# Two graph attention layers on one core: the uniform rows of two stages computed in one pair of records and spread through memory, with another order of the adjacency loads

## The chip, the cores and the metric

One core of one Trainium2 chip. The time is device microseconds of one execution; the median of several runs counts. Line numbers as L850 are lines of the kernel before. Stages are numbered from 0 to 15, and "late in stage 14" is a place in that numbering.

## What is computed

Eight graphs (B = 8) with 1024 nodes and 128 features each go through two layers. In each layer the features are normalised over a row, clipped at zero, projected with a 128 x 128 matrix, and combined by attention over the neighbours that the adjacency matrix (1.6% ones, int32) names; the result is added to the input. Layer 0 puts an ELU on the result, layer 1 doesn't.

```python
h  = maximum(layernorm(x), 0)
Wh = h @ W                                   # [8, 1024, 128]
e  = leaky_relu(Wh @ a1 [:, :, None] + Wh @ a2 [:, None, :], 0.2)
p  = softmax(where(adj > 0, e, very_negative), axis=2)
x  = x + elu(p @ Wh)                         # layer 1: x + p @ Wh
```

## The kernel before

**Stages.** A stage is one layer of one graph; 0 to 7 are layer 0, 8 to 15 (LAST) are layer 1. All engines run hand-written programs with semaphores between them, and work on neighbouring stages at once. While the matrix engine (PE) sums the attention of stage n, the projection of n+1 is made and the transposes of n+2.

**PE in stage n** (L954 to 961): `project(n + 1)`, eight matmuls of 130 columns (L850) and one more (L853) which multiplies the sum of the rows of h, repeated over 128 columns, by W; `attend(n, (0,))`, eight matmuls (L911) for mask 0; `spread_emax`, one transpose (L858); masks 1 to 5; eight transposes of stage n+2 (L789); masks 6 and 7. An f32 matmul is two records in the trace, so x16 is eight matmuls.

**Masks.** For each of the eight 128 x 1024 tiles of the adjacency VectorE (DVE) makes one operand of a matmul (L666): the larger of a row `row_r` that is the same on all partitions and a scalar, cut to the 0 or 1 of the adjacency by a minimum. To every sum a **uniform row** is added: `EMPTY` (2^-112) times the sum of all rows of Wh, so small that it counts only for a node without neighbours, whose softmax is uniform. Its first 128 columns are what L853 computes, on all partitions at once, into the free end of a bank of `prj` (`USUM`); DVE scales them into `uniform[:, m % 2, 0:D]` in `copy_e` (L602), and `copy_acc` (L675) of the same stage adds them as it moves the sums out of PSUM. A bank is free for PE's next stage only after that copy (`acc_copied`, waited for at L908).

**The row.** `row_r` of stage m comes from `sqr` (128 x 8, written by ScalarE, ACT, in `exps`), early in stage m-1: SP writes it to the DRAM tensor `r_rows` (L217), waits for that, and reads it back on all partitions as `row_by_node` (L222); ACT then puts it into the order of the masks with a stride of 8 elements (`sort_row`, L423), and DVE waits for that before mask 0 (L665). On ACT the copy `copy_hT(n + 2)` (L381), which the next `project` waits for, stands behind `sort_row`. Stage 1 alone does without memory (`SPREAD`).

**SP's queue.** One queue issues nearly all transfers, in the order written at L228 to 266, and stops at each wait. In iteration n it issues the adjacency tiles AHEAD (5) to 7 of stage n+1, the row's write and read (`load_row`), x of graph n+4 while there is one, tiles 0 to 4 of stage n+2, and in layer 1 the store of a finished graph. In iteration 1 tiles 5 to 7 come behind the row. The adjacency has three slots of eight tiles, and a load waits for the mask that used its tile three stages earlier.

**DVE in stage n** (L752 to 769): masks 0 and 1, `take_acc(n - 1)` (the three copies L675 and a reciprocal), `copy_e(n + 1)`, mask 2, `exp_args(n + 1)`, masks 3 to 5, the ELU and residual work, masks 6 and 7, statistics of n+3. Stage 15 has masks 0 and 1, `take_acc(14)`, then the rest.

## Time and profile before

| what | value |
|---|---|
| median of 3 runs | 296.29 us (295.84 to 296.66) |
| the profiled execution, its own time | 297.17 us |
| its span | 295.2 us |
| PE busy | 287.5 us, 97% of the span |
| DVE busy | 259.2 us, 88% |
| ACT busy | 190.5 us, 65% |
| the DMA queue that SP issues to | 82.78 MB, 74.4% of 16 engines |
| granted clock of PE | 1.0 of full speed |

The profiled execution took 0.88 us more than the median; the part of it outside the span (1.97 us) is launch and end. The page shows the span in equal slices, the chain of work that ended last, and groups of instructions. The trace behind it can be asked for the waits, the chain in order of time, a timeline by engine and busy time in windows.

### The profile page before, as it was taken

Reading aid. Unit: us, or ns where it says so; the run is one execution under the profiler, and the core shown is the slowest. Engines: PE = TensorE matmul, PEld = TensorE weight load, DVE = VectorE, ACT = ScalarE, POOL = GpSimd, SP = SyncE. Lnnn points to the kernel's source line nnn. Section 1 sums busy time; section 2 is a strip of 40 time slices with the busy share of each in tenths; the row PEclk is TensorE's granted clock in tenths of the full one; section 3 lists DMA queues with packets and bytes.
Section 4 is the critical chain, followed back from the end, with each engine's and each line's share of the span. In section 5 each row is a group of like instructions: output and inputs, shape, how many; then the busy total and the mean of one; then the engine's idle time right before and its main releaser. Section 6 shows DMA issues by size and latency. Waiting matters only on the chain.

```text
span 295.2 us, 6658 instructions
## 1 busy us (share of the span) xinstructions
PE 287.5 (97%) x2541; PEld 285.7 (97%) x2541; DVE 259.2 (88%) x538; ACT 190.5 (65%) x489; POOL 82.8 (28%) x157
## 2 busy tenths in 40 slices
PE   7999999997999999999999999999999999999796
PEld 7999999997999999999999999999999999999796
DVE  4798799887999999899898989888897979598786
ACT  3386786857958859585894968477475847743410
POOL 2722704314043160704316070512407051000000
PEclk9999999999999999999999999999999999999999
DMA  7999959969496987939496694948959598794012
GB/s 225 416 406 407 409 156 412 384 186 414 175 399 261 323 320 238 398 133 416 137 363 245 220 407 142 395 195 323 387 172 389 197 342 333 280 389 185 6 73 71
DMA packets 26383, 83.59 MB, mean 283 GB/s; under 512 B 4976, under 2 KB 6128, under 8 KB 26352
## 3 DMA queue, kind: packets, MB, share of 16 engines
q1 hardware_dynamic: 25776, 82.78, 74.4%
q10 hardware_dynamic: 576, 0.39, 0.4%
q8 instruction: 20, 0.33, 0.4%
q14 instruction: 11, 0.09, 0.1%
HBM read 78.91 MB, written 4.25 MB: 282 GB/s over the span
## 4 chain that ended last, share of the span: by engine, by line
PE 93%; DMA 3%; ACT 1%; DVE 1%; issue 0%; POOL 0%; POOLq 0%
PE acc L911 70%; PE prj L850 9%; PE tp L789 5%; PE acc L926 2%; DMA r_rows<-sqr 2%; PE acc L781 2%; DMA row_by_node<-r_rows 2%; PE prj L853 1%; ACT row_r L423 1%; PE prj L822 1%; PE tp L858 1%; PE prj L926 1%; PE prj L911 1%; PE acc L831 1%; DVE pbuf L666 0%; ACT wh L395 0%
## 5 line engine op out<-in xcount | busy, mean ns | idle before, releaser
L911 PE MATMUL acc<-wh,pbuf 128*128 128x129 f32 x1968 | 227.8, 275 | 1.7 <-DVE accs L675 1.5
L911 PEld LDWEIGHTS acc<-wh,pbuf 128*128 128x128 f32 x1968 | 223.9, 192 | 2.2 <-issue 1.9
L666 DVE SCALAR_TENSOR_TENSOR pbuf<-row_r,sqr,adj_sb 128x1024 f32<-128x1024 f32 x126 | 156.5, 1279 | 12.7 <-ACT row_r L423 12.7
L430 ACT ACTIVATE accs<-accs,rec 128x128 f32<-128x128 f32 x120 | 36.7, 389 | 42.0 <-DVE rec L685 42.0
L274 POOL TENSOR_TENSOR mean<-stats 128x8 f32<-128x8 f32 x14 | 9.7, 690 | 142.3 <-DVE stats L554 141.1
L375 ACT ACTIVATE xn<-x_sb,shift,rstd 128x128 f32<-128x128 f32 x120 | 47.7, 479 | 0.0
L423 ACT ACTIVATE row_r<-row_by_node 128x1024 f32<-128x1024 f32 x14 | 29.4, 2098 | 19.2 <-DMA row_by_node<-r_rows 19.2
L395 ACT ACTIVATE wh<-prj,wh 128x128 f32<-128x128 f32 x120 | 32.8, 365 | 0.0
L850 PE MATMUL prj<-w_ext,hT 128*128 128x130 f32 x240 | 29.4, 275 | 1.8 <-ACT hT L381 1.8
L850 PEld LDWEIGHTS prj<-w_ext,hT 128*128 128x128 f32 x240 | 28.0, 191 | 2.0 <-ACT hT L381 2.0
L303 POOL TENSOR_TENSOR rstd<-vareps,neg_half 128x8 f32<-128x8 f32 x15 | 26.9, 1791 | 6.8 <-DVE vareps L573 5.7
L554 DVE BATCH_NORM_STATS2 stats<-x_sb 128x6 f32<-128x128 f32 x112 | 23.0, 279 | 0.0
L675 DVE TENSOR_TENSOR accs<-acc,uniform 128x387 f32<-128x387 f32 (+1 forms) x45 | 20.5, 508 | 0.5 <-PE acc L911 0.4
L789 PE MATMUL tp<-ident,xn 128*128 128x128 f32 x128 | 17.2, 274 | 0.0
L381 ACT ACTIVATE hT<-tp 128x1024 f32<-128x1024 f32 x15 | 15.4, 1027 | 1.6 <-PE tp L789 1.6
L789 PEld LDWEIGHTS tp<-ident,xn 128*128 128x128 f32 x128 | 14.7, 141 | 0.5 <-ACT xn L337 0.3
L386 ACT ACTIVATE sqr<-args 128x24 f32<-128x24 f32 x15 | 3.3, 223 | 15.1 <-DVE args L632 15.1
L598 DVE COPY ecol<-prj 128x12 f32<-128x12 f32 x15 | 2.6, 171 | 10.6 <-PE prj L853 10.6
L277 POOL TENSOR_SCALAR negmean<-mean 128x8 f32<-128x8 f32 x14 | 10.7, 763 | 1.2
L696 DVE TENSOR_TENSOR x_sb<-x_sb,ex 128x1024 f32<-128x1024 f32 x8 | 9.8, 1220 | 0.0
L690 DVE SCALAR_TENSOR_TENSOR ex<-accs,ex 128x1024 f32<-128x1024 f32 x8 | 9.8, 1219 | 0.0
L442 ACT ACTIVATE ex<-ex 128x1024 f32<-128x1024 f32 x8 | 8.5, 1058 | 0.3
(102 smaller groups left out, 179.6 us busy)
## 6 DMA issues: line engine op xcount, KB each, us to landing
adj_sb<-in_adj SPq DMA_DIRECT2D x128, 512.0 KB, 9.3
row_by_node<-r_rows SPq DMA_DIRECT2D x14, 512.0 KB, 4.3
x_sb<-in_x SPq DMA_DIRECT2D x7, 512.0 KB, 8.4
out_x<-x_sb SPq DMA_DIRECT2D x7, 512.0 KB, 9.4
x_sb<-in_x ACTq DMA_DIRECT2D x1, 256.0 KB, 3.5
x_sb<-in_x SPq DMA_DIRECT2D x1, 256.0 KB, 3.3
r_rows<-sqr SPq DMA_DIRECT2D x14, 4.0 KB, 2.7
out_x<-x_sb SPq DMA_DIRECT2D x1, 192.0 KB, 1.9
```

The source lines that it names most:

```text
L303: nc.gpsimd.tensor_tensor(rstd[:, :], vareps[:, :], neg_half[:, :], ALU.pow).then_inc(rstd_ready, 1)
L375: nc.scalar.activation(xn[:, t, :], src[:, t, :], ACT.Identity, bias=shift[:, t:t + 1], scale=rstd[:, t:t + 1]).then_inc(xn_ready, 1)
L381: nc.scalar.activation(hT[:, :], tp[:, :], ACT.Relu, accum_out=hsum[:, :]).then_inc(hT_ready, 1)
L395: nc.scalar.activation(wh[:, m % 2, t, 0:D], prj[:, k, s * E:s * E + D], ACT.Copy, scale=wh[:, m % 2, t, D:C]).then_inc(wh_ready, 1)
L423: nc.scalar.activation(row_r[:, m % 2, :].rearrange("q (t p) -> q t p", t=T), row_by_node[:, :].rearrange("q (p t) -> q t p", t=T), ACT.Co ...
L430: op = nc.scalar.activation(hp[:, t, :], hp[:, t, :], ACT.Copy, scale=rec[:, t:t + 1])
L554: st = nc.vector.bn_stats(stats[:, t, :], src[:, t, :])
L666: nc.vector.scalar_tensor_tensor(pbuf[:, t, :], row_r[:, n % 2, :], sqr[:, n % 2, 0, t:t + 1], adj_at(n, t), ALU.max, ALU.min).then_inc(p_ ...
L675: nc.vector.tensor_tensor(accs[:, k * NB:k * NB + w, :], acc[:, k, 0:w * C].rearrange("p (s c) -> p s c", c=C), uniform[:, e % 2, :].unsqu ...
L789: return nc.tensor.transpose(tp[:, t * P:(t + 1) * P], xn[:, t, :], ident[:, :])
L850: nc.tensor.matmul(prj[:, k, s * E:(s + 1) * E], hT[:, t * P:(t + 1) * P], w_ext[:, l, :], start=(s == 0), stop=True, skip_group_check=True)
L911: mm = nc.tensor.matmul(sum_at(k, s), pbuf[:, t, i * P:(i + 1) * P], wh[:, n % 2, t, :], start=(t == 0 and s == 0 and k < NB), stop=(t == ...
```

## The change

1. **Uniform rows in pairs.** The matmul L853 goes from `project` for stages 2 to 15. ACT's `copy_hT(m)` leaves the sum of the rows of h in column m of `hsum`. For even n (2 to 14), after `project(n + 1)`, `usum_pair(n)` multiplies the two columns n and n+1 by W, with a result on 2 partitions (`UPAIR`, in the second bank of `tp`). ACT scales it into `u_sums` (2 x 128) in `copy_u(n)`, after `exps(n + 1)`. SP writes that to the DRAM tensor `u_rows` (`write_u`) and reads it back on all partitions straight into both halves of `uniform` (`read_u`), which waits for the write and for `take_acc(n - 1)`. `copy_acc(e, 0)` for e > 1, and `seed_last`, wait for that transfer (`u_in`); the transposes of stage n+2 wait for `copy_u`. DVE's L602 remains for stage 1 only.
2. **Order of SP's queue.** Ahead of the row of stage n+1 stand tiles 0 to 4 of stage n+1, and tiles 5 to 7 come behind it in every iteration; before, from iteration 2 on, all eight stood ahead.
3. **Mask 0 of stage 15** reads `row_by_node` itself, with the stride of 8, and waits for the transfer; mask 1 waits for ACT's sorted row.

Python's line numbers shift; the diff, without the declarations of semaphores and other lines that only follow:

```diff
--- before.py
+++ after.py
...
@@ -82,7 +80,8 @@
         q_rstd = sb("q_rstd", [P, T])
         xn = sb("xn", [P, T, D])
         hT = sb("hT", [P, T * P])
-        hsum = sb("hsum", [P, 1])
+        hsum = sb("hsum", [P, 2 * B])
+        u_sums = sb("u_sums", [2, D])
         wh = sb("wh", [P, 2, T, C])
         ecol = sb("ecol", [P, T, 2])
         emax = sb("emax", [P, 1])
@@ -105,6 +104,9 @@
         tp = ps("tp", [P, 2 * BANK])
         HSUM0 = acc[:, NB - 1, 0:1]
         WA = (prj[:, 0, 0:2], acc[:, 1, 0:2])
+        UPAIR = tp[0:2, BANK:BANK + D]
+        u_rows = nc.dram_tensor("u_rows", (2, D), F32, kind="Internal").ap()
         USUM = prj[:, NB - 1, tiles_in[-1] * E:tiles_in[-1] * E + D]
         w_in = [sem(f"w_in{l}") for l in range(2)]
...
...
@@ -220,6 +231,20 @@
                 if k > 1:
                     sp.wait_ge(row_sorted, k - 1)
                 sp.dma_start(row_by_node[:, :], line.partition_broadcast(P)).then_inc(row_in, 16)
+            def write_u(n):
+                k = n // 2
+                sp.wait_ge(u_copied, k)
+                if k > 1:
+                    sp.wait_ge(u_in, 16 * (k - 1))
+                sp.dma_start(u_rows, u_sums[:, :]).then_inc(u_written, 16)
+            def read_u(n):
+                sp.wait_ge(u_written, 16 * (n // 2))
+                sp.wait_ge(acc_copied, NB * n)
+                sp.dma_start(uniform[:, :, 0:D],
+                             u_rows.rearrange("s d -> (s d)").partition_broadcast(P)
+                             .rearrange("p (s d) -> p s d", s=2)).then_inc(u_in, 16)
             def store(b):
                 sp.wait_ge(hp_free, stage_of[1, b] + 1)
@@ -239,23 +264,26 @@
             for t in range(T):
                 load_adj(1, t)
             load_x(4)
-            for t in range(AHEAD):
+            for t in range(2):
                 load_adj(2, t)
             for n in range(1, LAST):
-                if n > 1:
-                    for t in range(AHEAD, T):
-                        load_adj(n + 1, t)
+                for t in range(2, 5):
+                    load_adj(n + 1, t)
                 load_row(n + 1)
-                if n == 1:
-                    for t in range(AHEAD, T):
-                        load_adj(n + 1, t)
+                if n % 2 == 0:
+                    write_u(n)
+                for t in range(5, T):
+                    load_adj(n + 1, t)
                 if n + 4 < B:
                     load_x(n + 4)
+                if n % 2 == 0:
+                    read_u(n)
                 if n + 2 <= LAST:
-                    for t in range(AHEAD):
+                    for t in range(2):
                         load_adj(n + 2, t)
                 if stages[n - 1][0] == 1:
                     store(stages[n - 1][1])
...
@@ -379,7 +407,7 @@
             def copy_hT(m):
                 act.wait_ge(tr_done, m + 1)
                 nc.scalar.activation(hT[:, :], tp[:, :], ACT.Relu,
-                                     accum_out=hsum[:, :]).then_inc(hT_ready, 1)
+                                     accum_out=hsum[:, m:m + 1]).then_inc(hT_ready, 1)
             def exps(m):
                 act.wait_ge(args_ready, m + 1)
@@ -424,6 +452,14 @@
                                      row_by_node[:, :].rearrange("q (p t) -> q t p", t=T),
                                      ACT.Copy).then_inc(row_sorted, 1)
+            def copy_u(n):
+                k = n // 2
+                act.wait_ge(upair_done, k)
+                if k > 1:
+                    act.wait_ge(u_written, 16 * (k - 1))
+                nc.scalar.activation(u_sums[:, :], UPAIR, ACT.Copy,
+                                     scale=EMPTY).then_inc(u_copied, 1)
             def scale_accs(e):
                 act.wait_ge(rec_ready, e + 1)
                 for t in range(T):
@@ -446,7 +482,8 @@
                 act.wait_ge(wh_ready, T * LAST + T)
-                act.wait_ge(e_copied, 3 * LAST + 3)
+                act.wait_ge(e_copied, e_copies(LAST))
+                act.wait_ge(u_in, 16 * (LAST // 2))
                 for k in range(len(last_parts) - NB):
                     nc.scalar.activation(prj[:, k, 0:C], uniform[:, LAST % 2, :],
                                          ACT.Copy).then_inc(seeded_last, 1)
@@ -482,6 +519,8 @@
                 scale_accs(n - 1)
                 if n < LAST:
                     exps(n + 1)
+                    if n % 2 == 0:
+                        copy_u(n)
                     if elu:
                         elu_exp(n - 1)
                     if n + 2 <= LAST:
@@ -599,9 +638,10 @@
                                       full).then_inc(e_copied, 1)
                 part = prj[:, 2, 0:tiles_in[2] * E].rearrange("p (s e) -> p s e", e=E)[:, :, D:E]
                 nc.vector.tensor_copy(ecol[:, 2 * NB:T, :], part).then_inc(e_copied, 1)
-                nc.vector.tensor_scalar(uniform[:, m % 2, 0:D], USUM, EMPTY, None,
-                                        ALU.mult).then_inc(e_copied, 1)
-                dve.wait_ge(e_copied, 3 * m + 3)
+                if m == 1:
+                    nc.vector.tensor_scalar(uniform[:, m % 2, 0:D], USUM, EMPTY, None,
+                                            ALU.mult).then_inc(e_copied, 1)
+                dve.wait_ge(e_copied, e_copies(m))
                 nc.vector.tensor_reduce(emax[:, :], ecol[:, :, 1], AX_X, ALU.max).then_inc(emax_ready, 1)
             def exp_args_first():
@@ -667,9 +707,24 @@
                                                    sqr[:, n % 2, 0, t:t + 1], adj_at(n, t),
                                                    ALU.max, ALU.min).then_inc(p_ready, 1)
+            def mask_unsorted(n):
+                dve.wait_ge(adj_in[n % ADJ_SLOTS][0], 16 * (n // ADJ_SLOTS + 1))
+                dve.wait_ge(p_used, n)
+                dve.wait_ge(row_in, 16 * loaded_rows(n))
+                nc.vector.scalar_tensor_tensor(
+                    pbuf[:, 0, :].rearrange("q (t p) -> q t p", t=T),
+                    row_by_node[:, :].rearrange("q (p t) -> q t p", t=T),
+                    sqr[:, n % 2, 0, 0:1],
+                    adj_at(n, 0).rearrange("q (t p) -> q t p", t=T),
+                    ALU.max, ALU.min).then_inc(p_ready, 1)
+                dve.wait_ge(row_sorted, loaded_rows(n))
             def copy_acc(e, k):
                 if k == 0 and e > 0:
                     dve.wait_ge(hp_free, e)
+                if k == 0 and e > 1:
+                    dve.wait_ge(u_in, 16 * (e // 2))
                 dve.wait_ge(acc_done, NB * e + k + 1)
                 w = tiles_in[k]
                 nc.vector.tensor_tensor(
@@ -767,7 +822,8 @@
                     masks(n, (6, 7))
                 if n + 3 <= LAST:
                     statistics(n + 3)
-            masks(LAST, range(DRAIN))
+            mask_unsorted(LAST)
+            masks(LAST, range(1, DRAIN))
             take_acc(LAST - 1)
             masks(LAST, range(DRAIN, 5))
             add_hp(B - 2)
@@ -809,6 +865,8 @@
                 else:
                     pe.wait_ge(cmax_ready, m)
                 pe.wait_ge(xn_ready, xn_before(m + 1))
+                if m > 3:
+                    pe.wait_ge(u_copied, (m - 2) // 2)
                 for t in range(T):
                     mm = turn(t)
                 mm.then_inc(tr_done, 1)
@@ -847,11 +905,20 @@
                     pe.wait_ge(e_copied, 3)
                     pe.wait_ge(wext_ready[1], 1)
                 for t, (k, s) in enumerate(bank_of):
-                    nc.tensor.matmul(prj[:, k, s * E:(s + 1) * E], hT[:, t * P:(t + 1) * P],
-                                     w_ext[:, l, :], start=(s == 0), stop=True,
-                                     skip_group_check=True)
-                nc.tensor.matmul(USUM, hsum[:, 0:1].to_broadcast([P, P]), w_ext[:, l, 0:D],
-                                 start=False, stop=True, skip_group_check=True).then_inc(prj_done, 1)
+                    mm = nc.tensor.matmul(prj[:, k, s * E:(s + 1) * E], hT[:, t * P:(t + 1) * P],
+                                          w_ext[:, l, :], start=(s == 0), stop=True,
+                                          skip_group_check=True)
+                if m == 1:
+                    mm = nc.tensor.matmul(USUM, hsum[:, m:m + 1].to_broadcast([P, P]),
+                                          w_ext[:, l, 0:D], start=False, stop=True,
+                                          skip_group_check=True)
+                mm.then_inc(prj_done, 1)
+            def usum_pair(n):
+                pe.wait_ge(hT_ready, n + 2)
+                nc.tensor.matmul(UPAIR, hsum[:, n:n + 2], w_ext[:, stages[n][0], 0:D], start=True,
+                                 stop=True, skip_group_check=True).then_inc(upair_done, 1)
             def spread_emax(m):
                 pe.wait_ge(emax_ready, m + 1)
@@ -953,6 +1020,8 @@
             attend(0, (7,))
             for n in range(1, LAST):
                 project(n + 1)
+                if n % 2 == 0:
+                    usum_pair(n)
                 attend(n, (0,))
                 spread_emax(n + 1)
                 attend(n, (1, 2, 3, 4, 5))
```

**SP's queue from the start of iteration 1 to the row of stage 4**, before and then after (`row_by_node` is the row on all partitions, `u_rows` and `uniform` the new pair of transfers):

```order
L210 DMA adj_sb<-in_adj 128x1024 x5
L217 DMA r_rows<-sqr 128x8
L222 DMA row_by_node<-r_rows 128x1024
L210 DMA adj_sb<-in_adj 128x1024 x3
L205 DMA x_sb<-in_x 128x1024
L210 DMA adj_sb<-in_adj 128x1024 x8
L217 DMA r_rows<-sqr 128x8
L222 DMA row_by_node<-r_rows 128x1024
L205 DMA x_sb<-in_x 128x1024
L210 DMA adj_sb<-in_adj 128x1024 x8
```

```order
L221 DMA adj_sb<-in_adj 128x1024 x5
L228 DMA r_rows<-sqr 128x8
L233 DMA row_by_node<-r_rows 128x1024
L221 DMA adj_sb<-in_adj 128x1024 x3
L216 DMA x_sb<-in_x 128x1024
L221 DMA adj_sb<-in_adj 128x1024 x5
L228 DMA r_rows<-sqr 128x8
L233 DMA row_by_node<-r_rows 128x1024
L240 DMA u_rows<-u_sums 2x128
L221 DMA adj_sb<-in_adj 128x1024 x3
L216 DMA x_sb<-in_x 128x1024
L245 DMA uniform<-u_rows 128x2x128
L221 DMA adj_sb<-in_adj 128x1024 x5
L228 DMA r_rows<-sqr 128x8
```

The row of stage 3 (second `r_rows` entry) had 3 + 8 tiles and an x behind the row of stage 2, and has 3 + 5 tiles and an x; three tiles moved behind it. The new write stands directly behind the row's read, and the new read behind three tiles and an x.

**SP's queue in iterations 13 and 14**, the last rows, before and after:

```order
L210 DMA adj_sb<-in_adj 128x1024 x5
L226 DMA out_x<-x_sb 128x1024
L210 DMA adj_sb<-in_adj 128x1024 x3
L217 DMA r_rows<-sqr 128x8
L222 DMA row_by_node<-r_rows 128x1024
L226 DMA out_x<-x_sb 128x1024 x2
```

```order
L221 DMA adj_sb<-in_adj 128x1024 x5
L251 DMA out_x<-x_sb 128x1024
L221 DMA adj_sb<-in_adj 128x1024 x3
L228 DMA r_rows<-sqr 128x8
L233 DMA row_by_node<-r_rows 128x1024
L240 DMA u_rows<-u_sums 2x128
L221 DMA adj_sb<-in_adj 128x1024 x3
L245 DMA uniform<-u_rows 128x2x128
L251 DMA out_x<-x_sb 128x1024 x2
```

Before, all tiles of stage 15 stood ahead of its row; now three stand behind it, between the new write and the new read, and the store comes last. In between the rows of stages 14 and 15 (the `x5`, the store and the `x3`) stand eight tiles and a store in both.

**PE, from the projection of stage 3 to that of stage 4 and beyond**, before and after:

```order
L911 MATMUL acc<-wh,pbuf 128x129 x16
L850 MATMUL prj<-w_ext,hT 128x130 x8
L853 MATMUL prj<-w_ext,hsum 128x128
L911 MATMUL acc<-wh,pbuf 128x129 x8
L858 MATMUL tp<-ident,emax 128x128
L911 MATMUL acc<-wh,pbuf 128x129 x40
L789 MATMUL tp<-ident,xn 128x128 x8
L911 MATMUL acc<-wh,pbuf 128x129 x16
L850 MATMUL prj<-w_ext,hT 128x130 x8
L853 MATMUL prj<-w_ext,hsum 128x128
L911 MATMUL acc<-wh,pbuf 128x129 x8
```

```order
L978 MATMUL acc<-wh,pbuf 128x129 x16
L908 MATMUL prj<-w_ext,hT 128x130 x8
L920 MATMUL tp<-w_ext,hsum 2x128
L978 MATMUL acc<-wh,pbuf 128x129 x8
L925 MATMUL tp<-ident,emax 128x128
L978 MATMUL acc<-wh,pbuf 128x129 x40
L845 MATMUL tp<-ident,xn 128x128 x8
L978 MATMUL acc<-wh,pbuf 128x129 x16
L908 MATMUL prj<-w_ext,hT 128x130 x8
L978 MATMUL acc<-wh,pbuf 128x129 x8
L925 MATMUL tp<-ident,emax 128x128
```

Of the matmuls after the eight of a projection every second one is gone, and the others have two weight columns and stand in `tp`.

**DVE at the turn from stage 14 to stage 15**, before and after:

```order
L702 TENSOR_TENSOR x_sb<-accs,x_sb 128x1024
L666 SCALAR_TENSOR_TENSOR pbuf<-row_r,sqr,adj_sb 128x1024 x4
L675 TENSOR_TENSOR accs<-acc,uniform 128x387 x2
L675 TENSOR_TENSOR accs<-acc,uniform 128x258
L685 RECIPROCAL rec<-accs 128x8
```

```order
L757 TENSOR_TENSOR x_sb<-accs,x_sb 128x1024
L706 SCALAR_TENSOR_TENSOR pbuf<-row_r,sqr,adj_sb 128x1024 x2
L715 SCALAR_TENSOR_TENSOR pbuf<-row_by_node,sqr,adj_sb 128x1024
L706 SCALAR_TENSOR_TENSOR pbuf<-row_r,sqr,adj_sb 128x1024
L730 TENSOR_TENSOR accs<-acc,uniform 128x387 x2
L730 TENSOR_TENSOR accs<-acc,uniform 128x258
L740 RECIPROCAL rec<-accs 128x8
```

The first mask of stage 15 now reads `row_by_node`; its place is the same.

## Rows read from the trace of the kernel before

**Rows 1.** The page, its span and the busy share of the matrix engine

```profile
span 295.2 us, 6658 instructions
...
PE 287.5 (97%) x2541; PEld 285.7 (97%) x2541; DVE 259.2 (88%) x538; ACT 190.5 (65%) x489; POOL 82.8 (28%) x157
```

**Rows 2.** The waits: engine, line, for whom; us in total, times, longest us

```profile
PE prj L850 <- ACT hT L381: 1.8, 1, 1.8
...
PE acc L911 <- DVE accs L675: 1.5, 1, 1.5
```

**Rows 3.** The chain in order of time, around stage 3: start us, us, what

```profile
55.61 5.28 DMA r_rows<-sqr
...
60.91 4.45 DMA row_by_node<-r_rows
...
69.54 2.05 PE prj L850 x16
```

**Rows 4.** The timeline of ScalarE before stage 3: start us, us, instruction, [idle before]

```profile
65.38 2.08 ACT L423 ACTIVATE row_r<-row_by_node 128x1024 f32<-128x1024 f32 x1 [3.34 <-DMA row_by_node<-r_rows]
```

**Rows 5.** The chain again, matmuls at start-up and in stage 4

```profile
9.94 0.89 PE acc L831 x8
...
88.88 0.22 PE prj L853 x2
```

**Rows 6.** Windows: busy us (count) by engine, clock, DMA share, GB/s

```profile
55.60:58.80 3.20, 3.20 (x31) 3.20 (x30) 3.20 (x3) 3.15 (x7) 0.00 (x0) 1.00 0.95 371
58.80:61.30 2.50, 2.50 (x25) 2.50 (x24) 2.50 (x4) 2.50 (x8) 0.00 (x0) 1.00 0.09 25
252.00:255.00 3.00, 3.00 (x29) 3.00 (x28) 2.64 (x3) 1.23 (x5) 0.00 (x0) 1.00 0.77 242
255.00:258.00 3.00, 3.00 (x29) 3.00 (x29) 0.40 (x1) 2.62 (x2) 0.00 (x0) 1.00 1.02 408
```

**Rows 7.** The timeline of SP's queue, stages 12 and 14: the row's two transfers

```profile
230.53 0.33 SPq L217 DMA_DIRECT2D r_rows<-sqr  x1
234.16 0.33 SPq L222 DMA_DIRECT2D row_by_node<-r_rows  x1
...
265.10 0.33 SPq L217 DMA_DIRECT2D r_rows<-sqr  x1
268.14 0.33 SPq L222 DMA_DIRECT2D row_by_node<-r_rows  x1
```

**Rows 8.** The page, part 6: transfers, KB each, us from issue to landing

```profile
row_by_node<-r_rows SPq DMA_DIRECT2D x14, 512.0 KB, 4.3
...
r_rows<-sqr SPq DMA_DIRECT2D x14, 4.0 KB, 2.7
out_x<-x_sb SPq DMA_DIRECT2D x1, 192.0 KB, 1.9
```

**Rows 9.** The timeline at the start of stage 13

```profile
242.42 1.87 PEld L850 LDWEIGHTS prj<-w_ext,hT 128*128 128x128 f32 x16
...
242.99 1.35 DVE L675 TENSOR_TENSOR accs<-acc,uniform 128x387 f32<-128x387 f32 x3
```

**Rows 10.** The timeline at the start of stage 15

```profile
272.59 2.07 ACT L423 ACTIVATE row_r<-row_by_node 128x1024 f32<-128x1024 f32 x1 [5.07 <-DMA row_by_node<-r_rows]
...
274.79 2.48 DVE L666 SCALAR_TENSOR_TENSOR pbuf<-row_r,sqr,adj_sb 128x1024 f32<-128x1024 f32 x2 [2.87 <-ACT row_r L423]
277.19 1.02 DVE L675 TENSOR_TENSOR accs<-acc,uniform 128x387 f32<-128x387 f32 x2
...
277.89 0.35 PE L911 MATMUL acc<-wh,pbuf 128*128 128x129 f32 x1 [1.50 <-DVE accs L675]
```

**Rows 11.** The page, part 5: groups of equal size, busy us, mean ns of one

```profile
L666 DVE SCALAR_TENSOR_TENSOR pbuf<-row_r,sqr,adj_sb 128x1024 f32<-128x1024 f32 x126 | 156.5, 1279 | 12.7 <-ACT row_r L423 12.7
...
L423 ACT ACTIVATE row_r<-row_by_node 128x1024 f32<-128x1024 f32 x14 | 29.4, 2098 | 19.2 <-DMA row_by_node<-r_rows 19.2
...
L442 ACT ACTIVATE ex<-ex 128x1024 f32<-128x1024 f32 x8 | 8.5, 1058 | 0.3
```

More of the change, by code:

```diff
@@ L33, in gat_two_layers @@
     DRAIN = 2
-    AHEAD = 5
     bank_of = [(i // NB, i % NB) for i in range(T)]
@@ L129, in gat_two_layers @@
         usum_done = sem("usum_done")
+        upair_done = sem("upair_done")
+        u_copied = sem("u_copied")
+        u_written = sem("u_written")
+        u_in = sem("u_in")
         q_rstd_ready = sem("q_rstd_ready")
@@ L194, in loaded_rows, with e_copies @@
             return len([k for k in range(1, m + 1) if k not in SPREAD])
+        def e_copies(m):
+            return 3 * m + 3 if m < 2 else 2 * m + 4
         def xn_before(m):
@@ L346, in copy_hsum_first @@
                 act.wait_ge(hsum_done, 1)
-                nc.scalar.activation(hsum[:, :], HSUM0, ACT.Copy).then_inc(hsum_ready, 1)
+                nc.scalar.activation(hsum[:, 0:1], HSUM0, ACT.Copy).then_inc(hsum_ready, 1)
             def copy_row_first(h):
```

## The prediction

> **What bounds the kernel now.** I read the page first: PE is busy for 287.5 of 295.2 us [rows 1]. So only two things can give time back: work taken from PE, and the few waits in which PE stands still. The waits name two of them behind the start-up: 1.8 us of `project` for `hT`, and 1.5 us of the attention sums for DVE's copy of the accumulators [rows 2]. The chain in order of time tells where the first is: the row of stage 3 is written at 55.61, which takes 5.28 us, is read in 4.45 us, and only at 69.54 can PE project [rows 3]. ACT had been idle for 3.34 us before it sorted that row at 65.38, so it was ready at 62.04 [rows 4], and `copy_hT` stood behind the sort. The second wait is at the start of stage 15: ACT sorts the row at 272.59, DVE makes masks 0 and 1 from 274.79, copies the accumulators from 277.19, and PE goes on at 277.89, after 1.50 us [rows 10]. Everywhere else an engine other than PE can lose or gain some tenths of a microsecond without a trace at the end.
>
> **The matmuls.** L853 is one f32 matmul, two records, 0.22 us of the chain [rows 5]. Of the 14 that go (stages 2 to 15), seven come back as `usum_pair`, so PE is rid of seven. The pair's matmul has 2 weight columns instead of 128, with the same 128 moving columns. Its price is between 0 and 0.22 us. A nearby row: four matmuls (eight records) with 128 weight columns and a single moving one took 0.89 us, 0.22 each [rows 5], the same as L853, so the weights alone account for 0.22 us, and what 128 moving columns cost with few weights isn't seen. I take 0.22, the row with the same moving operand. That gives 7 x 0.22 = 1.5 us, and at the lower end, with pairs for nothing, 3.1. The Trainium skill (TensorE: Matmul & The Clock Gate, Back-to-back issue gap) speaks for less than 0.22: it gives 81 ns as the spacing of a stream of load and matmul pairs at 128 columns and 56 ns for a matmul without its load budget. By that ratio a pair would cost 0.15 us, and seven of them would save another 0.5 us. What PE waits for at its pair is `copy_hT(n + 1)`, which `project(n + 1)` has just waited for, so nothing.
>
> **DVE and ACT.** DVE loses 14 scalings of 128 x 128, ahead of `emax`, which PE asks for only after the eight matmuls of mask 0; that hides it before, so it is worth nothing now. ACT gets seven copies on 2 partitions, a few tenths each at most, while it waits in most stages for the row; only where `copy_hT` is tight would they be seen. The transposes wait for `copy_u`, which comes nearly 10 us before them. Nothing for these.
>
> **Stage 3's wait.** Three tiles fewer stand between the rows of stages 2 and 3. A tile is 0.52 MB, and a full queue moves 408 GB/s [rows 6], so the queue is 3 x 0.52 / 408 = 3.8 us less behind when the write is issued. Before, it was full for 3.2 us after the issue, and then all but empty for 2.5 us, in which only the write was still to land [rows 6]. So 5.3 us becomes about 2 (of all 14 such writes the median is 2.7 [rows 8], full queues included). The row lands at 55.6 + 2 + 4.3 [rows 8] = 61.9, when ACT is ready, 3.3 us sooner than before. PE needs 1.8 us of that; the stall goes until the write takes more than 3.7 us. Worth 1.8 us, between 0 and 1.8. The following rows profit a little and were not late for PE.
>
> **How late the queue will be in layer 1.** Here the order doesn't help: between two rows there are eight tiles and a store as before. What is added is u's read of 0.13 MB, 0.3 us at 408 GB/s; while a row is being copied to all partitions the queue moves only 242 GB/s [rows 6], so I take 0.5. And every second stage is 0.22 us shorter. Before, write to read took 3.63 us in stage 12 and 3.04 us in stage 14 [rows 7]. With two pairs (10 and 12) that fall into a full queue, some 0.7 each, less what slack stage 10 still has, the row of stage 15 is issued about 1 us later: 265.10 + 4.0 = 269.1, where before it was 268.14. Ends: 3.04 (no change) and 4.7.
>
> **The new wait, u's round trip.** `take_acc(n)` must have it. The write stands behind the row's read, and lands about with it, 4.3 us after the row's issue. The read then is behind three tiles. While the row is being copied, the queue moves 242 GB/s x 3 us = 0.73 MB [rows 6], the row and 0.2 MB of tiles; the remaining 1.37 MB take 3.3 us. u is at 7.6 us, and its own 0.13 MB and its landing take between 0.3 us (its bytes) and 2.9 (a row's 4.3 less some 1.4 before its data flow). A store of 192 KB takes 1.9 us with its issue and landing when nothing is ahead of it [rows 8], so I take 0.9, about half of that. So u lands 8.5 us after the row's issue, between 7.9 and 10.5.
>
> For all pairs but the last PE has a margin. At the start of stage 13 PE's projection began at 242.42 and the copies at 242.99 [rows 9], which cost PE nothing. PE asks for the first bank 1.8 us after that start, and the copy takes 0.5, so the copy may begin 1.3 us after it: 243.7, or 13.2 us after the write was issued at 230.53 [rows 7]. u comes 3.6 + 8.5 = 12.1 us after, or 13 with the drift: in time. Nothing, and 0.3 us in stage 13 or so at the upper end. In stage 2, with x in the queue too (1.3 us), it is 2 + 8.5 + 1.3 = 11.8.
>
> **Stage 15.** Without u the third part would do its work: mask 0 from 272.6 (the row's landing), mask 1 after the sort at 274.8, `take_acc` at 276.05 instead of 277.19, just as PE ends its bank (PE's pause begins at 277.89 - 1.50 = 276.39, the copy can start 0.34 earlier): 1.1 us. ACT's strided sort takes 2098 ns and a contiguous pass of the same size 1058 [rows 11], so the stride may cost on DVE too: mask 0 then takes between 1279 ns [rows 11] and twice that, which is 0.1 us at the end, since mask 1 waits for the sort in any case; I take nothing. The Trainium skill (SBUF — State Buffer, Door 1: The DMA port swizzle) has the rule to that: each access to another line of 16 bytes pays a penalty, and a stride of 8 f32 values is 32 bytes. ACT's two rows agree, and by it mask 0 would be slow. But `take_acc(14)` now waits for u: 269.1 + 8.5 = 277.6, that is 0.4 us later than the 277.19 before. DVE makes the last masks just in time for PE, so the end moves with `take_acc`. I take -0.4 us: what the third part gives, u takes. Ends: 268.14 + 7.9 = 276.04 gives +1.1; 269.8 + 10.5 = 280.3 gives -3.1.
>
> **Sum:** 1.5 + 1.8 - 0.4 = 2.9 us less. The profiled execution has 297.17, which becomes 294.3; it lies 0.9 us above the median of 296.29, for which I forecast 293.4.
>
> **The rivals.**
> *U in time (18%).* The queue is no fuller than before and u lands at 7.9: the last stage gives 1.1. 1.5 + 1.8 + 1.1 = 4.4, 291.9 us. For it: transfers of bytes alone are short. Against it: the full queue of layer 1.
> *Cheap pairs (12%).* The load sets the pace of a matmul and 2 columns load in next to nothing; a pair costs the middle of its two ends, 0.11: 0.8 more, 3.7 in all, 292.6. For it: [rows 5] leave the moving side open. Against it: a matmul with one moving column is no shorter than one with 128 there, so both sides may be equally long. (The page on TensorE named above leans this way.)
> *A fuller queue (12%).* The row is issued 4.7 us after the write and u lands 9.5 us after that: -2.1 in stage 15 (279.3 for 277.19) and -1.0 at the pair 12 (14.2 us after the write for 13.2). 3.3 - 3.1 = 0.2, 296.1 us.
> *Stage 3 stays (5%).* The write of its row is late for its landing, not for what is ahead of it: 1.1 less, 295.2. The empty 2.5 us speak for it, the 3.2 full ones against it.
> *The round trip becomes the clock (5%): slower.* Place: the wait of `copy_acc` for u at each of the seven pairs. It decides from a landing some 10.5 us after the row's issue. At 11.5 with a write of 2.7 us, the median, it is past the 13.2 us by 1.0 at the pairs 4 to 10, by 1.6 at pair 2 (a write of 2 us, and x), by 1.9 at pair 12 (3.6), and 3.4 late in stage 15: 10.9 lost against 3.3 gained, 303.9 us. For it: a read that waits for a write in memory, behind a queue that is full. Against it: 2.7 and 4.3 us for the row's own two steps [rows 8].
>
> **The numbers.** The forecast has 48%. The range of 291.7 to 295.3 takes in *in time*, *cheap pairs* and *stage 3 stays*, and the forecast with its late u; outside are most of *fuller* and all of *slower*. A measurement here tells 0.3%, 0.9 us, from no change. Faster by more: 48 + 18 + 12 + 4 and a third of *fuller*, 86%. Within: 8%. Slower: 6%.
>
> **What would show it.** Right: no wait of PE for `hT` near 68 us, the second row's write at 2 us; the seven pair matmuls at about 0.11 us a record in the chain; in stage 15 a wait of `accs` for the transfer `uniform`, after which PE resumes at about the same distance from its last matmul as before, 1.5 to 2 us; elsewhere no wait of PE. Wrong: waits of PE for the copies in stages 3, 5, 7 and on (the round trip is slow), or DVE's copies of stage 15 released by mask 1 (u was in time).

## The result and the profile after

| | median us | runs |
|---|---|---|
| before | 296.48 | 295.84 to 296.92, 4 |
| the change | 300.47 | 299.90 to 302.11, 4 |

The ratio is 1.0126, with a 95% interval of 1.0076 to 1.0176: the change is slower, by 4.0 us, where 2.9 us faster was forecast. The profiled execution took 299.93 us, 2.8 more than that of before. Medians and ratios here and below leave out the executions that were in the slower state of the chip; the first profile of e5_order_only was of one (603.5 us), which is why that kernel was run again.

From the page after (span, busy shares, the chain by engine, and the row's write in the list of transfers):

```profile
span 298.1 us, 6657 instructions
...
PE 289.8 (97%) x2527; PEld 285.4 (96%) x2527; DVE 256.9 (86%) x524; ACT 191.6 (64%) x496; POOL 81.9 (27%) x157
...
PE 83%; DMA 13%; DVE 2%; issue 1%; SPq 0%; ACT 0%; POOL 0%; DVEq 0%; POOLq 0%
...
r_rows<-sqr SPq DMA_DIRECT2D x14, 4.0 KB, 2.5
```

PE has fewer instructions and is busy for longer than in [rows 1]. 13% of the chain that ended last are now transfers, where before it was 3%. The waits (us in total, times, longest):

```profile
DVE accs L730 <- DMA uniform<-u_rows: 7.9, 6, 2.3
...
PE acc L978 <- DVE accs L730: 3.8, 3, 2.5
```

The wait of PE for `hT` [rows 2] isn't there any more; in its place PE waits three times for DVE's copies, and DVE waits for `uniform`: at six of the seven pairs, of which three reach PE. The chain in order of time shows the first of them, at the start of stage 3:

```profile
55.86 2.40 DMA r_rows<-sqr
...
58.65 3.09 DMA u_rows<-u_sums
...
61.75 8.24 DMA uniform<-u_rows
...
70.07 0.57 DVE accs L730
```

The write of the row takes 2.40 us where it took 5.28 [rows 3], as the order of the loads should make it. But the chain doesn't go on with the row. It goes through the write of u and its read, which lands at 69.99: 11.7 us after the row's issue at 58.28 (SP's issue of the row's read, as in the prediction). The same at stage 13 (10.9 us, PE waits 0.36) and at stage 15. There, SP's queue and then the timeline of DVE and PE:

```profile
268.51 0.33 SPq L233 DMA_DIRECT2D row_by_node<-r_rows  x1
269.27 0.24 SPq L240 DMA_DIRECT2D u_rows<-u_sums  x1
269.56 1.29 SPq L221 DMA_DIRECT2D adj_sb<-in_adj  x3
271.63 0.38 SPq L245 DMA_DIRECT2D uniform<-u_rows  x1
```

```profile
273.27 2.11 DVE L715 SCALAR_TENSOR_TENSOR pbuf<-row_by_node,sqr,adj_sb 128x1024 f32<-128x1024 f32 x1 [0.96 <-DMA row_by_node<-r_rows]
275.30 1.28 DVE L706 SCALAR_TENSOR_TENSOR pbuf<-row_r,sqr,adj_sb 128x1024 f32<-128x1024 f32 x1
278.59 1.36 DVE L730 TENSOR_TENSOR accs<-acc,uniform 128x387 f32<-128x387 f32 x3 [2.01 <-DMA uniform<-u_rows]
...
279.29 2.83 PE L978 MATMUL acc<-wh,pbuf 128*128 128x129 f32 x12 [2.52 <-DVE accs L730]
```

Row issued at 268.51, u's read at 271.63, landed at 278.5, which is 10.0 us after the row. Masks 0 and 1 were ready at 276.6, and DVE stood still for 2.01 us. PE goes on at 279.29, after 2.52 us, where before it was 277.89 after 1.50 [rows 10]. What follows wasn't in any step. The windows after that wait (busy us of PE, PEld, DVE, ACT, POOL with counts, then granted clock, DMA share, GB/s), and the chain there:

```profile
280.00:281.00 1.00, 1.00 (x6) 1.00 (x6) 1.00 (x2) 0.78 (x3) 0.00 (x0) 0.50 0.00 0
281.00:282.00 1.00, 1.00 (x7) 1.00 (x6) 1.00 (x2) 1.00 (x5) 0.00 (x0) 0.50 0.03 8
282.00:283.00 1.00, 1.00 (x7) 1.00 (x7) 1.00 (x2) 0.67 (x3) 0.00 (x0) 0.60 0.00 0
```

```profile
279.29 2.83 PE acc L978 x12
282.13 0.83 PE prj L978 x4
282.96 1.34 PE acc L978 x12
```

The same place in the chain of before:

```profile
277.89 1.58 PE acc L911 x12
279.47 0.45 PE prj L911 x4
```

The granted clock falls to 0.50, the lower of its two levels (1.2 of 2.4 GHz), and the first 16 records of stage 15 take 3.66 us where before 16 took 2.03 (1.58 and 0.45): 1.6 us lost.

The pairs, in the chain at stage 4 and, without a pair, at stage 5:

```profile
88.08 0.31 PE tp L920 x2
88.39 1.98 PE acc L978 x16
...
105.66 1.79 PE acc L978 x16
```

L853 took 0.22 us and the 16 records behind it 1.79, as in the chain of before at stage 4:

```profile
88.88 0.22 PE prj L853 x2
89.10 1.79 PE acc L911 x16
```

A pair takes 0.31, and the 16 records behind it 1.98: it costs 0.50, not 0.22. The timeline of the weight loads shows where the second part comes from, first of the change, then of before at the same place:

```profile
88.01 0.09 PEld L920 LDWEIGHTS tp<-w_ext,hsum 128*2 128x2 f32 x2
88.32 0.63 PEld L978 LDWEIGHTS acc<-wh,pbuf 128*128 128x128 f32 x5 [0.22 <-issue]
```

```profile
88.72 0.39 PE L853 MATMUL prj<-w_ext,hsum 128*128 128x128 f32 x2
88.83 1.31 PEld L911 LDWEIGHTS acc<-wh,pbuf 128*128 128x128 f32 x11
```

The next load of 128 columns starts only at 88.32, when the pair's two records are all but through (88.39 in the chain), and the loads had been idle for 0.22 us. Before, it started at 88.83, while the records of L853 (88.72 to 89.11) were still running.

**The account** of the two profiled executions, along PE's chain: start-up +0.2; seven pairs +0.28 each and seven projections without L853 -0.22 each, +0.4; the wait for `hT` -1.8; the waits for copies 3.8 for 1.5, +2.3; the lower clock +1.6. That makes +2.7, of +2.9 in the spans.

### The profile page after: what moved, and what is told of

Same layout as the page of the kernel before. It is cut to its first block, busy times and chain, and to the rows that moved or that the text cites. A ratio compares the mean times of both kernels' runs of the same rounds, so it can differ in the third digit from the quotient of the medians.

```text
span 298.1 us, 6657 instructions
## 1 busy us (share of the span) xinstructions
PE 289.8 (97%) x2527; PEld 285.4 (96%) x2527; DVE 256.9 (86%) x524; ACT 191.6 (64%) x496; POOL 81.9 (27%) x157
## 4 chain that ended last, share of the span: by engine, by line
PE 83%; DMA 13%; DVE 2%; issue 1%; SPq 0%; ACT 0%; POOL 0%; DVEq 0%; POOLq 0%
PE acc L978 62%; PE prj L908 8%; DMA uniform<-u_rows 8%; PE tp L845 4%; DMA u_rows<-u_sums 3%; DMA r_rows<-sqr 3%; PE acc L993 2%; PE acc L837 2%; PE tp L920 1%; PE prj L978 1%; PE prj L880 1%; PE tp L925 1%; PE prj L993 1%; DVE accs L730 1%; PE acc L889 1%
## 5 line engine op out<-in xcount | busy, mean ns | idle before, releaser
L302 POOL TENSOR_TENSOR mean<-stats 128x8 f32<-128x8 f32 x14 | 11.6, 828 | 142.7 <-DVE stats L593 141.5
L331 POOL TENSOR_TENSOR rstd<-vareps,neg_half 128x8 f32<-128x8 f32 x15 | 26.0, 1730 | 6.9 <-DVE vareps L612 5.8
L305 POOL TENSOR_SCALAR negmean<-mean 128x8 f32<-128x8 f32 x14 | 13.2, 940 | 1.2
L663 DVE TENSOR_REDUCE cmax<-tp 128x1 f32<-128x128 f32 x15 | 4.4, 291 | 6.6 <-PE tp L925 6.5
```

The lines of the kernel that those rows point to most:

```text
L331: nc.gpsimd.tensor_tensor(rstd[:, :], vareps[:, :], neg_half[:, :], ALU.pow).then_inc(rstd_ready, 1)
```

## The experiments

Medians belong to each kernel's own runs; ratios are to the kernel before on the same chip. Labels are those of the expectations.

**e1_no_pairs: the change without its first part**

```diff
-                if n % 2 == 0:
-                    usum_pair(n)
...
-                if m == 1:
-                    mm = nc.tensor.matmul(USUM, ...)
+                mm = nc.tensor.matmul(USUM, ...)
```

> The change without its first part: each projection keeps its own matmul for the uniform row, no transfer of u; the order of the loads and the unsorted mask stay. Theory (the loss is all in the pairs: their matmuls, the wait for u, the clock after it): no wait of PE for hT near 68 us, PE's wait at the start of stage 15 0.3 to 0.5 us instead of 1.5, no fall of the granted clock; about 3 us (1.8 and 1.1) under the kernel before, ratio 0.990. Rival (the new order of the loads makes the queue late in layer 1, and the pairs only show it): the row's writes in stages 12 and 14 take 4 us and more, PE still waits over 1.5 us at stage 15, ratio above 0.995.

294.29 us, ratio 0.9907 (0.9865 to 0.9948), which is the theory's number: order and mask together give 2.7 us, and all the loss is in the pairs. Two signs of the rival showed up in the profile all the same. PE still waited for 1.78 us at stage 15, since the row's read there took 5.45 us to land instead of 4.3, and the row's write took 4.0 and 4.6 us in stages 11 and 12 (3.4 in stage 14). The profiled execution was the slowest of the eight (296.21 us), and the ratio isn't the rival's. The clock stayed at 1.0.

**e2_wide_pair: 128 weight columns**

```diff
-                nc.tensor.matmul(UPAIR, hsum[:, n:n + 2], ...
+                nc.tensor.matmul(UWIDE, hsum[:, n:n + P], ...
...
```

> As the change, but the pair's matmul has 128 weight columns (two used, the others zeros or sums of other stages) and writes 128 partitions; transfers and waits as in the change. Theory (a matmul with 2 weight columns between ones with 128 costs 0.50 us: 0.31 of its own and 0.19 because the next load can't run beside it): the pair takes 0.22 us in the chain and the 16 records behind it 1.79 instead of 1.98, so 0.28 less per pair, 2.0 us of PE work in all; the time falls by less, 1 to 2 us, as the waits for u grow by what PE gains ahead of them. Rival (the cost comes from the place of the pair in tp or from its semaphore, not from its 2 columns): 0.31 and 1.98 stay.

```profile
225.37 0.22 PE tp L922 x2
225.59 1.79 PE acc L980 x16
```

The chain has 0.22 and 1.79 us, so the price of the pair came from its 2 columns, as the theory said. The time did not follow: 300.34 us, ratio 1.0117 (1.0041 to 1.0194), as slow as the change. Its profile has more of the waits:

```profile
PE acc L980 <- DVE accs L732: 7.1, 3, 5.1
```

5.1 of these 7.1 us are at stage 15, where the row's write took 4.2 us and u's read 8.2. While u sets the end, work taken from PE only makes the wait longer.

**e3_u_first: u right behind the row**

```diff
                 sp.dma_start(line..., sqr[:, m % 2, 2, :]).then_inc(r_written, 16)
+                if m % 2 == 1:
+                    write_u(m - 1)
                 sp.wait_ge(r_written, 16 * k)
...
                 sp.dma_start(row_by_node[:, :], ...).then_inc(row_in, 16)
+                if m % 2 == 1:
+                    read_u(m - 1)
...
```

> As the change, but u is written directly behind the row's write and read directly behind the row's read, ahead of the three tiles (and x). Theory (u is late since its read stands behind the row's landing and three tiles): u lands 5 to 7 us after the row's issue instead of 10.0 to 11.7, no wait of DVE for it, PE's waits at stages 3 and 13 gone and the one at stage 15 under 0.6 us, the granted clock stays at 1.0 there: 4 to 4.5 us less than the change, about the time of the kernel before or 0.5 under it. Rival (the read of u is slow in itself, 256 pieces of 512 bytes out of one place in memory): u still lands 8 us or more after the row, and waits stay. Rival 2 (an early read takes its time from the tiles, the queue is late and the rows too): row writes over 4 us in stages 12 and 14.

SP's queue in iteration 14:

```profile
263.91 0.33 SPq L228 DMA_DIRECT2D r_rows<-sqr  x1
264.34 0.25 SPq L244 DMA_DIRECT2D u_rows<-u_sums  x1
267.55 0.32 SPq L235 DMA_DIRECT2D row_by_node<-r_rows  x1
267.97 0.37 SPq L249 DMA_DIRECT2D uniform<-u_rows  x1
```

The landing of u from its read's issue, in the change and here:

```profile
DMA to landing us min/median/max: 6.3/7.0/8.2
DMA to landing us min/median/max: 4.9/5.1/5.3
```

So u lands 5.3 to 5.7 us after the row's issue, and PE has no wait for it, nor for anything else behind the start-up. The row's writes in stages 12 to 14 take 2.3, 3.9 and 3.6 us (2.7, 3.6 and 3.0 in the change), so none is over 4. 295.06 us, ratio 0.9945 (0.9918 to 0.9972): by the ratios 5.4 us under the change, with nothing moved but these two transfers, and 1.9 under the kernel before, more than I expected. The first theory holds in its mechanism, and both rivals fall.

**e4_warm: PE kept busy in the last wait**

```diff
+            pe.wait_ge(u_copied, LAST // 2)
+            for _ in range(22):
+                nc.tensor.transpose(tp[:, BANK:BANK + P], ident[:, :], ident[:, :])
             attend(LAST, range(LAST_SPLIT))
```

> As the change, with 22 transposes of the identity in PE's wait before the sums of stage 15 (0.11 us each, 2.4 us, the length of the wait). Theory (the clock falls to half because PE stands still for 2.5 us there, and the first 16 records of stage 15 then cost 3.66 us instead of 2.03): the granted clock stays at 1.0 at 279 to 283 us, those records take 1.3 and 0.45 us, 1.6 us less in the profiled run. Rival (the fall has nothing to do with the wait): the clock falls at the same place and the time stays within 0.3 us.

```profile
277.47 2.56 PE L1033 MATMUL tp<-ident 128*128 128x128 f32 x22
280.81 1.58 PE L978 MATMUL acc<-wh,pbuf 128*128 128x129 f32 x12 [0.78 <-DVE accs L730]
```

With the transposes in the wait, the clock stays at 1.0, and the first 16 records take 2.03 us (1.58 and 0.45) again. From where PE goes on to the end of its work are 14.65 us, in the change 16.19, so 1.5 us come back. With PE busy in the wait the clock doesn't fall, which makes the standstill the cause. The time is no better, 301.08 us, ratio 1.0137 (1.0077 to 1.0197). In this execution u landed 1.5 us later (280.0 for 278.5): the row's write was issued 0.9 us later (266.34 for 265.48; PE had waited for 1.38 us at stage 5), and the row's write and u together took 0.6 us longer. My expectation of the time failed by the scatter of these other waits.

The mean granted clock that is on record for every execution tells more, since a fall of this length lowers it to 0.994. In the change three of four executions had that or less, here one of four. The clock also fell in executions of the kernel before: 11 of the 72 that the experiments had beside them stand at 0.994, with a median of 298.6 us against 296.7 for the rest. So it did in 5 of the 18 of the second part alone (e5, e12). With the third part and no late u (e1, e3, e6, e9, e11, e13) it was none of 48. So part of the kernel's own scatter is this fall. Where it lies in executions without a trace isn't shown.

**e5_order_only and e12_order_again: the second part alone** (one kernel, run twice)

```diff
-                if n > 1:
-                    for t in range(AHEAD, T):
-                        load_adj(n + 1, t)
+                for t in range(2, 5):
+                    load_adj(n + 1, t)
                 load_row(n + 1)
...
+                for t in range(5, T):
+                    load_adj(n + 1, t)
...
```

> The kernel before with the change's second part alone (the order of the loads). Theory (the order removes the wait of PE for hT at stage 3, 1.8 us, and does nothing in layer 1): the row of stage 3 is written in 2 to 2.7 us instead of 5.3, no wait of PE near 68 us, ratio to before 0.993 to 0.995. Rival (the later row writes get slower by it, as a look at layer 1 in the version without pairs suggests, where the write of stage 11 took 4.6 us): waits of PE of 1 us or more in stages 10 to 15, ratio 0.996 to 1.0.

> The same kernel as e5_order_only, whose profile was of a disturbed execution. Theory: the write of stage 3's row takes 2 to 2.7 us, no wait of PE for hT at stage 3, span 1.5 to 1.9 us under that of before but for what stage 15 differs. Rival: the writes of the rows of stages 11 to 15 take over 4 us and PE waits more at stage 15 than the 1.5 us of before, which takes back most of it, ratio 0.997 to 1.0.

Ratios 0.9970 (0.9931 to 1.0010) and 0.9957 (0.9924 to 0.9991); medians 295.29 and 295.51 us. The profile of the second has the row of stage 3 written in 2.4 us, no wait for `hT`, and a span of 293.4, 1.8 under before. In layer 1 the writes take 2.8, 3.5 and 3.4 us in stages 12 to 14, where before it was 3.6, 3.3 and 3.0: none over 4, and no clear change. The wait at stage 15 is 1.8 for 1.5 us:

```profile
PE acc L909 <- DVE accs L673: 1.8, 1, 1.8
```

The theory holds in the profile. The intervals alone allow anything between 0 and 2 us, but much of the scatter is the clock: by the means of those executions of both kernels whose granted clock is 0.999 or more, this kernel is 1.6 us under the one before in the first run and again in the second.

**e11_mask_only: the third part alone**

```diff
...
-            masks(LAST, range(DRAIN))
+            mask_unsorted(LAST)
+            masks(LAST, range(1, DRAIN))
```

> The kernel before with the change's third part alone. The unsorted mask takes 2.1 us on DVE instead of 1.28, and mask 1 still waits for ACT's sort; without a wait for u the copies of stage 15 begin 1.1 us sooner. Theory: PE's wait at stage 15 is 0.3 to 0.5 us instead of 1.5, ratio to before 0.996. Rival (the wait at stage 15 follows the row's landing, and the strided mask gives back its gain): wait over 1.2 us, ratio 1.0.

```profile
275.28 1.35 DVE L688 TENSOR_TENSOR accs<-acc,uniform 128x387 f32<-128x387 f32 x3
...
275.98 1.24 PE L925 MATMUL acc<-wh,pbuf 128*128 128x129 f32 x9 [0.28 <-DVE accs L688]
```

PE's wait is 0.28 us instead of 1.50, with a mask 0 of 2.11 us. 295.48 us, ratio 0.9952 (0.9925 to 0.9978). The third part is worth 1.2 us in the profile, if u isn't waited for, and none of its ten executions had the lower clock. Order and mask alone, 0.9957 and 0.9952, make 0.991 together, the 0.9907 of e1_no_pairs.

**e6_pairs_no_dma: pairs without their transfers.** Left out: the write and read of u and the waits for it, so the uniform rows of stages 2 to 15 are those of the first two.

> The change with its pair matmuls and ACT's copies, but without the two transfers of u and the waits for them; the uniform rows of stages 2 to 15 are those of stages 0 and 1. Theory (a pair costs 0.50 us on PE, the rest of the loss is the wait for the transfers and the clock): the version without pairs has 14 x 0.22 = 3.1 us in their place and this one 7 x 0.50 = 3.5, so this one is 0.4 slower than that, ratio to before 0.991 to 0.993, with no wait of PE over 1.8 us and no fall of the clock. Rival (my price of 0.22 was right and the waits are all): 1.5 us less than without pairs, ratio 0.985.

293.94 us, ratio 0.9908 (0.9871 to 0.9945), where e1_no_pairs had 294.29. At 0.22 a pair it would be 1.5 us under that, a ratio of 0.985, which is outside its interval. The chain has 0.31 and 1.98 here too, by which seven pairs cost 3.5 us and fourteen L853 3.1; a difference that small the intervals of over 1 us can't tell. The saving of PE's work that the first part was to bring is nil even if its transfers cost nothing.

**e7_one_piece: one piece of 1032 bytes per partition**

```diff
-                sp.dma_start(uniform[:, :, 0:D], ...)
+                sp.dma_start(uniform[:, :, :].rearrange("p s c -> p (s c)"), ...)
```

> As the change, but u has 129 columns and is read as one piece of 1032 bytes per partition, not two of 512. Theory (the read's own part is long because of its 256 small pieces): u lands 1 us or more sooner (median of 7.0 us from the read's issue falls under 6), waits of PE for the copies fall by as much, 1 to 2 us less in all. Rival (its place behind the tiles and the landing set it): median of 6.7 to 7.3, the same time within noise, 300 to 301 us.

Median landing 7.2 us (7.0 with two pieces), 300.29 us, ratio 1.0094 (1.0057 to 1.0132). The rival holds: the size of the pieces isn't what makes u late.

**e10_hold_tiles: nothing issued behind u's read until it lands**

```diff
                 sp.dma_start(uniform[:, :, 0:D], ...).then_inc(u_in, 16)
+                sp.wait_ge(u_in, 16 * (n // 2))
```

> As the change, but SP issues nothing behind the read of u until u has landed. From the row's issue u takes 10.0 to 11.7 us in the change, where a row (4.3), the rest of three tiles (3.3) and the 1.2 us that the read needs behind a row when u goes first make 8.8. Theory A (transfers issued later share the 16 engines with the read, so it isn't served in the order of issue): the median from the read's issue falls from 7.0 to 5.5 us or less. Theory B (in a full queue the last of 16 engines is 1 to 2 us behind the others, and the read waits for it): the median stays at 6.5 or more. In both the tiles come later and the rows of layer 1 with them; the time is as in the change or worse.

Median landing 6.4 us, between the two. At the first five pairs it is 1.6, 0.2, 0.7, 1.8 and 0.3 us shorter than in the change (6.6 for 8.2 at the first), so transfers issued later do delay the read, by an uneven amount. Only the first pair is a clean comparison, since from there on the held loads change what else is in the queue. The time is 313.0 us, ratio 1.0554 (1.0496 to 1.0611), with row writes of up to 8.1 us: an SP that waits for a landing starves the loads. Neither theory is clean. Some 6 us remain with nothing issued behind the read; e3_u_first, with only a row ahead, has 5.1.

**e9_wide_first: both repairs** (e2_wide_pair and e3_u_first together)

> The pair with 128 weight columns together with u written and read with the row, both repairs. Theory (two separate losses, the price of the 2-column matmul and the place of u in the queue): PE has 2.0 us less to do than with u first alone, of which layer 1 keeps some back, since its rows are written 3.5 to 3.9 us after the issue already: 1 to 2 us less than u first, ratio to before 0.985 to 0.991. Rival (layer 1 is at the pace of the queue, PE work no longer counts): the same as u first, 0.9945.

293.46 us, ratio 0.9900 (0.9861 to 0.9938), a span of 291.1 against 292.5 of e3_u_first. 1.4 us less in the spans and 1.3 by the ratios, so most of the 2.0 us of PE work come out at the end; at stage 15 PE waits for the copies for 0.75 us, where e3_u_first has no wait, and that is the rest. The intervals of the two overlap. It beats the kernel before and the change. It can't be told from e1_no_pairs (294.29), which has none of the transfers.

**e13_pair32: 32 weight columns, with u first**

```diff
-                nc.tensor.matmul(UPAIR, hsum[:, n:n + 2], ...
+                nc.tensor.matmul(UWIDE, hsum[:, n:n + 32], ...
```

> As the kernel with u first, but the pair's matmul has 32 weight columns and 32 partitions of result. With 2 columns the pair takes 0.31 us in the chain and the 16 records behind it 1.98; with 128 it takes 0.22 and 1.79. Theory A (any weight tile that isn't the whole 128 columns keeps the next load from running beside it): 0.31 and 1.98 again, the time of u first (295.1, ratio 0.9945). Theory B (the length of the load matters, a very short one leaves nothing to hide behind): 32 columns lie between, 0.25 and 1.85 or so.

```profile
261.27 0.33 PE tp L922 x2
261.60 1.98 PE acc L980 x16
```

0.33 and 1.98, 295.30 us, ratio 0.9948 (0.9927 to 0.9970). Theory A: a weight tile of 32 columns is as dear as one of 2, and the whole 128 are cheap. Widths between 32 and 128 weren't run, and the partitions of the result go with the width in all three, so which of the two counts isn't shown.

## Why the prediction was wrong

Between the two profiled executions 2.9 us less were forecast, and the spans show 2.9 more: a miss of 5.8 us. The matmuls make 1.9 of it, u's landing 1.3 at stages 3 and 13 and 0.6 at stage 15, the clock 1.6, the start-up 0.2; 0.2 are left.

**The matmuls** failed as a term and as a range. I took 0.22 us for a pair, "the row with the same moving operand", with ends of 0 and 0.22. The pair costs 0.50, more than the upper end, since I priced the instruction by itself and not what it does to its neighbour. +0.4 us instead of -1.5 is 1.9 us of the miss. e2, e6 and e13 show it. The rival *cheap pairs* erred the same way. The Trainium skill's ratio (TensorE: Matmul & The Clock Gate, Back-to-back issue gap), by which I put 0.15 beside it, is given for a stream of load and matmul pairs. The runs don't agree with it for a small matmul alone between others, which cost 0.50 us.

**The round trip** failed in size, and its margin was thin. The mechanism stood in the prediction; the term of 8.5 us was mis-sized. The step "u lands 8.5 us after the row's issue, between 7.9 and 10.5" measured 9.7 to 10.9 us, and 11.7 with x. In stage 15 the write landed 3.1 us after the row's issue, sooner than my 4.3, so it didn't set the time; the read did, 6.9 us from its issue. I had the tiles ahead of it gone at 7.6 us, 0.9 for its own part, the half of a lone store's 1.9, and nothing for transfers issued after it; e10 gives that last one 0.2 to 1.8 us, and behind a row alone (e3) the own part is 1.2 us (5.5 for the row's 4.3). With nothing behind, stage 3 in e10 has 10.0 us from the row's issue, where my terms with x make 9.8, and the other pairs 8.5 to 10.2, where they make 8.5: up to 1.7 us of those isn't resolved. The 13.2 us of margin from the row's write were right: outside stage 15, PE's wait is what the landing lies beyond them. Two pairs of the change did (2 and 12, at 14.1 and 13.5 us), which cost 1.0 and 0.4 us; pair 2 of e2 waited 1.3 us with a landing at 14.5, and that of e7 1.6 at 14.8.

**Stage 15** was to lose 0.4 us and lost 1.0 in the wait (2.52 us for 1.50), plus the clock. Here there was no margin at all, and I knew it: u at 277.6 against copies at 277.19. The row's write took 3.0 us, 1.0 less than the 4.0 I had taken, but u landed 10.0 us after the row's issue, for my 8.5. That a wait of 2.5 us can cost 1.6 more by the clock stood in no step and no rival. e4 shows it.

**Stage 3's wait** was right: a write of 2.4 for the 2 forecast, and the stall gone. It was replaced by u's wait at the same place, which takes back half. **The third part** was right in mechanism (mask 0 of 2.11 us, inside its 1.28 to 2.56; 1.2 us without u, where 1.1 was worked out), and as forecast u hid it. The rule of the Trainium skill on 16-byte lines (SBUF — State Buffer, Door 1: The DMA port swizzle) is borne out in its direction, 1.65 times the contiguous 1.28.

**The queue in layer 1** was no fuller than before: the row's write took 3.0 us in stage 14, where I took 4.0 and had 3.04 as the lower end. Since PE was slower, it wasn't put to the test; in e2, with less work for PE, it took 4.2.

**The rivals.** What happened is *the round trip becomes the clock* in kind, with 5%, but only in three of seven places; its price per place was too high and its point of decision, 10.5 us, about right. The range left it out. The chance was too small. I gave the landing one value and asked whether that was in time, though no row of before shows a small transfer that lands from within a full queue, and the margin to the copies was 1.1 us.

## What to carry to other kernels

When the matrix engine is the bound, price an added matmul by the spacing of its neighbours as well: one with 2 weight columns between full ones cost 0.50 us against 0.22, and padding it to 128 columns brought it to 0.22. A value that goes through memory and back is only as early as its place in the queue; put write and read beside a transfer that already makes that trip (5.4 us by two moved transfers), and not behind bulk loads that it doesn't need. A wait on such an engine may cost more than its length, if the clock falls with it; look at the granted clock behind the longer ones. Of the waits of PE in these profiles, behind the start-up, all six from 2.3 to 5.1 us had a fall and none of those up to 1.8. When the times of one kernel scatter, sort them by their mean granted clock before comparing.

## What the runs showed of the hardware that was not expected

- A pair's weight load of 2 or of 32 columns among loads of 128: 0.31 and 0.33 us for the two records instead of 0.22, and the next full load starts only when they are all but through, 0.19 us more on the 16 records behind.
- The granted clock fell from 1.0 to 0.50 with an idle time of PE of 2.52 us (2.26 in e7_one_piece, 5.12 in e2_wide_pair, 2.70, 3.46 and 2.71 in e10_hold_tiles), and was at 1.0 again only in the window from 283, over 3 us after PE went on. After waits of 1.78 and 1.79 us in e1 and e12 it stayed at 1.0.
- A read of 1 KB to all partitions took 5.1 us from its issue with a row ahead of it, and 7.0 (6.3 to 8.2) with three tiles; there, pieces of 1032 bytes (7.2) were no better than pieces of 512.
- DVE's pass with one operand at a stride of 8 f32 values took 2.11 us for 1.28; ACT's took 2.10 for the 1.06 of a contiguous pass of the same size.
